# A two-layer graph network on one core: router logits in one product, one attention product moved behind the second aggregation, and a tail written tile by tile

## The reference

```python
# layer 0: gnn0 = diffusion over the edges, mix0 = linear attention, ffn0 = 16 experts, 2 per node
x = x + gnn0(ln(x)) + mix0(ln(x))
x = x + ffn0(ln(x))              # gates: softmax(ln(x) @ w_gating)
# layer 1
xn = ln(x)
h  = xn + elu(ln(gat_conv(xn, W1, 8 heads)))
g  = h  + elu(ln(gat_conv(h,  W2, 1 head)))      # gat_conv: segment softmax over the edges, then sum
q, k, v = split(xn @ W_qkv); q = softmax(q, features); k = softmax(k, nodes)
mix = (q @ (k.T @ v)) @ W_out + b_out            # per head; k.T @ v is the "context"
x = x + g + mix
x = x + ffn1(ln(x))              # 8 experts, 2 per node; gates: softmax(ln(x) @ Wr + br)
```

## Time and profile before

| | us |
|---|---|
| three runs | 227.12, 228.76, 228.8 |
| median | 228.76 |
| the profiled execution, whole | 225.84 |
| its span, first to last instruction | 224.1 |
| TensorE busy in it | 212.0 |

### The profile page before, as it was taken

How to read it: one execution, slowest core, us unless ns; L and a number is a source line. 1 busy time by engine, 2 the same in 40 slices (tenths; PEclk the granted TensorE clock), 3 DMA queues, 4 the chain that set the end, 5 groups by cost and what they waited for, 6 DMA issues and landing times.

```text
span 224.1 us, 2899 instructions
## 1 busy us (share of the span) xinstructions
PE 212.0 (95%) x1008; PEld 140.5 (63%) x1008; DVE 140.5 (63%) x416; ACT 63.9 (28%) x150; POOL 21.2 (9%) x36
## 2 busy tenths in 40 slices
PE   7999999998999999999999999999969999499994
PEld 5785546654579688744845686469754444359741
DVE  3799999968997151332519139696944749734302
ACT  2804594231311112100011139930563202104100
POOL 4850100000101000000140000000300002100000
PEclk9999999999999999999997999999999999999999
DMA  6999899924050500000079200000000000000002
GB/s 170 346 391 350 265 414 412 407 81 146 6 184 3 187 0 3 0 0 0 0 244 389 118 0 1 3 0 0 0 0 3 0 0 0 0 1 3 0 0 94
DMA packets 8957, 23.65 MB, mean 106 GB/s; under 512 B 2408, under 2 KB 2408, under 8 KB 8944
## 3 DMA queue, kind: packets, MB, share of 16 engines
q1 hardware_dynamic: 8656, 23.42, 28.9%
q10 hardware_dynamic: 288, 0.07, 0.1%
HBM read 22.95 MB, written 0.52 MB: 105 GB/s over the span
## 4 chain that ended last, share of the span: by engine, by line
PE 84%; DVE 11%; issue 2%; POOL 0%; ACT 0%; POOLq 0%; DVEq 0%
PE bank L1158 17%; PE bank L1132 13%; PE bank L1250 10%; PE bank L1262 9%; PE bank L1298 6%; PE bank L1207 3%; PE bank L1169 3%; PE bank L1213 3%; DVE ring L792 3%; PE bank L1312 2%; PE bank L1146 2%; PE bank L1214 2%; PE bank L1198 2%; DVE ring L795 2%; PE bank L1444 1%
## 5 line engine op out<-in xcount | busy, mean ns | idle before, releaser
L1158 PE MATMUL bank<-raw,xT 128*128 128x512 f32 x88 | 39.9, 602 | 0.0
L1158 PEld LDWEIGHTS bank<-raw,xT 128*128 128x128 f32 x88 | 16.7, 195 | 19.2 <-issue 19.0
L303 POOL TENSOR_TENSOR rstd<-veps,minus_half 128x1 f32<-128x1 f32 x14 | 8.4, 607 | 158.8 <-DVE veps L569 90.3
L1250 PE MATMUL bank<-xT,raw 128*128 128x256 f32 x96 | 22.7, 386 | 0.0
L1298 PE MATMUL bank<-iota_bf 128*128 128x256 bf16 x144 | 21.1, 300 | 1.6 <-DVE iota_bf L768 1.6
L1262 PE MATMUL bank<-raw,ring 128*128 128x512 f32 x48 | 21.0, 594 | 0.0
L792 DVE TENSOR_SCALAR ring<-iota_bf,edges,radix 128x128 bf16<-128x128 bf16 x64 | 20.0, 379 | 0.0
L1250 PEld LDWEIGHTS bank<-xT,raw 128*128 128x128 f32 x96 | 17.6, 190 | 3.1 <-issue 0.9
L1298 PEld LDWEIGHTS bank<-iota_bf 128*128 128x128 bf16 x144 | 15.5, 112 | 5.1 <-DVE iota_bf L768 1.6
L1262 PEld LDWEIGHTS bank<-raw,ring 128*128 128x128 f32 x48 | 9.0, 190 | 10.9 <-issue 10.5
L1207 PE MATMUL bank<-raw,yT 128*128 128x512 f32 x32 | 14.3, 595 | 0.7 <-issue 0.7
(11 more groups left out here) (255 smaller groups left out, 331.8 us busy)
## 6 DMA issues: line engine op xcount, KB each, us to landing
raw<-in_up SPq DMA_DIRECT2D x6, 512.0 KB, 10.3
raw<-in_down SPq DMA_DIRECT2D x6, 512.0 KB, 13.0
raw<-in_k SPq DMA_DIRECT2D x4, 512.0 KB, 6.0
raw<-in_q SPq DMA_DIRECT2D x4, 512.0 KB, 6.7
raw<-in_v SPq DMA_DIRECT2D x4, 512.0 KB, 7.9
raw<-in_out SPq DMA_DIRECT2D x4, 512.0 KB, 6.5
raw<-in_gat SPq DMA_DIRECT2D x4, 512.0 KB, 9.1
raw<-in_gnn SPq DMA_DIRECT2D x2, 512.0 KB, 11.4
```

The lines of the kernel that those rows point to most:

```text
L1158: ins = mm(bank[banks[t]][:, :], xT_at(c, t), w.at(c), start=c == 0, stop=c == C - 1)
L1250: ins = mm(half(m // 2, m % 2), w.at(c, m * P, (m + 1) * P), xT_at(c), start=c == 0, stop=c == C - 1)
```

## The change

1. **Gates of both layers.** `logit_rows`, the ScalarE copy and the transposes go. `logits` now makes the logits in their final form, one tile at a time: the transposed rows are the stationary operand, and the gate weights (16 or 8 columns) stream. For layer 0 tile 0 stands right behind `xT_made(1)`, then five idle turns, then tile 1; for layer 1 both stand behind the five idle turns that follow `xT_made(4)`.
2. **`attention_weights` of the second `gat_conv`.** Four products in all. Chunk 0 goes ahead of the first `attn_out` of layer 0, chunks 1 and 2 to the place where chunk 0 and nine idle turns stood, and chunk 3 stays behind the experts of layer 0, among idle turns of other counts.
3. **`context` and `yT_made` of layer 1** go from ahead of `xT_made(3)` to behind the second aggregation, with six idle turns behind each. On ScalarE the copies of `ctxbd` and `yT` go along, ahead of the exponentials of the second elu. `h2` now lives in `hx` and `mixed` of layer 1 in `q`, since `ek` and `v` are still needed.
4. **VectorE's tail of layer 1** is written tile by tile in another order, instead of both tiles in each step.

The diff, cut to its core:

```diff
-        h2 = ek
+        h2 = hx[:, :, :, :].rearrange("p t h n -> p t (h n)")[:, :, 0:D]
...
             elu(0, (0,))
-            act.wait_ge(ctx_full, 2)
-            for r in range(2):
-                p0, p1 = r * HD, (r + 1) * HD
-                copy(ctxbd[p0:p1, :, p0:p1], bank[3][p0:p1, :].rearrange("p (m n) -> p m n", m=C)[:, :, p0:p1])\
-                    .then_inc(ctx_ready, 1)
             elu(0, (1,))
-            yT_part(1, (5, 2))
             xT_part(3, 4)
...
                 copy(h2[:, t, :], bank[5 - t][:, :]).then_inc(hx_ready, 1)
+            act.wait_ge(ctx_full, 2)
+            for r in range(2):
+                p0, p1 = r * HD, (r + 1) * HD
+                copy(ctxbd[p0:p1, :, p0:p1], bank[4][p0:p1, :].rearrange("p (m n) -> p m n", m=C)[:, :, p0:p1])\
+                    .then_inc(ctx_ready, 1)
+            yT_part(1, (5, 4))
             elu(1)
             xT_part(4, 3)
-            lgT_part(1, 5)
...
-            go(V.scalar_tensor_tensor(mixed[:, :, :], x1g[:, :, :], -1.0, xa[:, :, :], ALU.add, ALU.add))
+            go(V.scalar_tensor_tensor(q[:, :, :], x1g[:, :, :], -1.0, xa[:, :, :], ALU.add, ALU.add))
...
+            def negative(t):
+                settle()
                 dve.wait_ge(elu_exp, T + t + 1)
+                go(V.scalar_tensor_tensor(q[:, t, :], g_b[:, t, :], 1.0, q[:, t, :], ALU.min, ALU.add))
...
+            def summed(t):
+                settle()
                 dve.wait_ge(o_full, 2 + t + 1)
+                go(V.tensor_tensor(xb[:, t, :], bank[t][:, :], q[:, t, :], ALU.add))
                 settle()
                 variance(6, t, xb[:, t, :])
...
+            scaled(0)
+            settle()
+            variance(5, 0, g_a[:, 0, :])
+            scaled(1)
+            centred(0)
+            normal(0)
+            variance(5, 1, g_a[:, 1, :])
+            centred(1)
+            positive(0)
+            normal(1)
+            negative(0)
+            summed(0)
+            positive(1)
+            negative(1)
+            norm_rows(6, xn[:, 0, :], xb[:, 0, :], 0)
+            summed(1)
+            norm_rows(6, xn[:, 1, :], xb[:, 1, :], 1)
...
-            def logit_rows(b, L, i):
...
+            def logits(b, L, i, tiles=range(T)):
                 E = EXPERTS[L]
+                for t in tiles:
+                    pe.wait_ge(xT_ready[t], i + 1)
+                    ins = product(bank[b][:, N + t * E:N + (t + 1) * E], lambda c: xT_at(c, t),
+                                  lambda c: (w_router if L else w_gate)[:, c, 0:E], C)
+                if t == T - 1:
+                    ins.then_inc(logits_full, 1)
...
             yT_made(0, (4, 5))
+            pe.wait_ge(small_in, SMALLS)
+            attention_weights(1, 6, 0)
...
             diffuse(1, (3, 4))
-            attention_weights(1, 6, 0)
-            idle_turns(5, 9)
+            attention_weights(1, 6, 1)
+            idle_turns(5, 1)
+            attention_weights(1, 6, 2)
+            idle_turns(5, 1)
...
-            idle_turns(2, 6)
             pe.wait_ge(wa_ready, 1)
-            logit_rows(6, 0, 1)
-            up("up0", 0, 1, (0, 1))
-            logits(6, 0)
+            logits(6, 0, 1, (0,))
+            idle_turns(2, 5)
+            logits(6, 0, 1, (1,))
+            up("up0", 0, 4)
...
-            attention_weights(1, 7, 1)
-            idle_turns(5, 5)
-            attention_weights(1, 7, 2)
-            idle_turns(5, 2)
+            idle_turns(5, 6)
+            attention_weights(1, 7, 3).then_inc(wa_full, 1)
+            idle_turns(5, 6)
             xT_made(2, xn, (4, 5), (0,))
-            attention_weights(1, 7, 3).then_inc(wa_full, 1)
+            idle_turns(5, 4)
             xT_made(2, xn, (4, 5), (1,))
...
             qT_made((4, 5))
+            pe.wait_ge(qT_ready, 2 + C)
+            xT_made(3, x1g, (4, 3), (0,))
             pe.wait_ge(ek_ready, 4)
-            context(3)
-            pe.wait_ge(ctx_ready, 4)
-            pe.wait_ge(qT_ready, 2 + C)
-            yT_made(1, (5, 2))
-            xT_made(3, x1g, (4, 3))
+            xT_made(3, x1g, (4, 3), (1,))
...
+            context(4)
+            idle_turns(0, 6)
+            pe.wait_ge(ctx_ready, 4)
+            yT_made(1, (5, 4))
+            idle_turns(0, 6)
             pe.wait_ge(yT_ready, 4)
             for t in range(T):
                 attn_out("out1", t).then_inc(o_full, 1)
-            idle_turns(4, 4)
+            idle_turns(4, 8)
             xT_made(4, xn, (3, 4), (0,))
```

More of the change, by code:

```diff
@@ L371, in yT_part @@
                         .then_inc(yT_ready, 1)
-            def lgT_part(L, b):
-                act.wait_ge(lgT_full, L + 1)
-                copy(lgT[0:EXPERTS[L], :], bank[b][0:EXPERTS[L], 0:N]).then_inc(lgT_ready, 1)
             def gate_exp(L):
@@ L436, in _ @@
             copy(wa[:, :, 0:2 * H], bank[6][:, 0:C * A2].rearrange("p (c n) -> p c n", c=C)[:, :, 0:2 * H])
-            copy(wa[:, 0, 2 * H:A2], bank[6][:, 2 * H:A2]).then_inc(wa_ready, 1)
-            lgT_part(0, 6)
+            copy(wa[:, 0:3, 2 * H:A2], bank[6][:, 0:C * A2].rearrange("p (c n) -> p c n", c=C)[:, 0:3, 2 * H:A2])\
+                .then_inc(wa_ready, 1)
             gate_exp(0)
@@ L473, in _ @@
             act.wait_ge(wa_full, 2)
-            copy(wa[:, 1:C, 2 * H:A2], bank[7][:, 0:C * A2].rearrange("p (c n) -> p c n", c=C)[:, 1:C, 2 * H:A2])\
-                .then_inc(wa_ready, 1)
+            copy(wa[:, 3, 2 * H:A2], bank[7][:, 3 * A2 + 2 * H:4 * A2]).then_inc(wa_ready, 1)
             xT_part(2, 4)
@@ L1088, in _ @@
                     .then_inc(weight_ready, 1)
-            go(V.scalar_tensor_tensor(mixed[:, :, :], x1g[:, :, :], -1.0, xa[:, :, :], ALU.add, ALU.add))
+            go(V.scalar_tensor_tensor(q[:, :, :], x1g[:, :, :], -1.0, xa[:, :, :], ALU.add, ALU.add))
             settle()
-            go(V.tensor_tensor(mixed[:, :, :], mixed[:, :, :], row["b_out1"].unsqueeze(1).broadcast_to([P, T, D]),
+            go(V.tensor_tensor(q[:, :, :], q[:, :, :], row["b_out1"].unsqueeze(1).broadcast_to([P, T, D]),
                                ALU.add))
@@ L1097, in _, with scaled @@
             settle()
-            for t in range(T):
+            def scaled(t):
                 dve.wait_ge(agg_full, 4 + t + 1)
@@ L1101, in _, with centred, normal, positive @@
                                           ALU.mult, ALU.add))
-            gat_norm(1, 5)
-            for t in range(T):
+            def centred(t):
+                go(V.scalar_tensor_tensor(g_a[:, t, :], g_a[:, t, :], mv[:, t, 0:1], row["g2"],
+                                          ALU.subtract, ALU.mult))
+                settle()
+            def normal(t):
+                dve.wait_ge(rstd_ready, T * 5 + t + 1)
+                V.scalar_tensor_tensor(g_a[:, t, :], g_a[:, t, :], rstd[:, t:t + 1], row["beta2"],
+                                       ALU.mult, ALU.add).then_inc(y_ready, 1)
+            def positive(t):
                 dve.wait_ge(y_ready, T + t + 1)
-                go(V.scalar_tensor_tensor(mixed[:, t, :], g_a[:, t, :], 0.0, mixed[:, t, :], ALU.max, ALU.add))
-            for t in range(T):
-                settle(T - 1)
+                go(V.scalar_tensor_tensor(q[:, t, :], g_a[:, t, :], 0.0, q[:, t, :], ALU.max, ALU.add))
+            def negative(t):
+                settle()
                 dve.wait_ge(elu_exp, T + t + 1)
-                go(V.scalar_tensor_tensor(mixed[:, t, :], g_b[:, t, :], 1.0, mixed[:, t, :], ALU.min, ALU.add))
-            for t in range(T):
-                settle(T - 1 if t == 0 else 0)
+                go(V.scalar_tensor_tensor(q[:, t, :], g_b[:, t, :], 1.0, q[:, t, :], ALU.min, ALU.add))
+            def summed(t):
+                settle()
                 dve.wait_ge(o_full, 2 + t + 1)
-                go(V.tensor_tensor(xb[:, t, :], bank[t][:, :], mixed[:, t, :], ALU.add))
+                go(V.tensor_tensor(xb[:, t, :], bank[t][:, :], q[:, t, :], ALU.add))
                 settle()
                 variance(6, t, xb[:, t, :])
-                norm_rows(6, xn[:, t, :], xb[:, t, :], t)
+            scaled(0)
+            settle()
+            variance(5, 0, g_a[:, 0, :])
[13 more added lines that the diff above has]
+            norm_rows(6, xn[:, 1, :], xb[:, 1, :], 1)
             xT_part(4, 4)
@@ L1544, in _ @@
             idle_turns(6, 5)
[L1545 to L1549, removed]
+            logits(5, 1, 4)
+            up("up1", 0, 2)
             up("up1", 2, 3, (0, 1))
```

5 lines of the change are left out of this document (removed).

## The result

| | before | changed |
|---|---|---|
| median, us | 227.94 (20 runs) | 228.56 (20 runs) |
| lowest and highest | 223.90, 230.50 | 226.53, 242.11 |
| changed / before | | 1.0084, 95% interval 1.0043 to 1.0125 |

The forecast was 227.5 us, faster by 0.6%; by the ratio the kernel is slower, and only the range held the time.

A forecast was written before the change was run, and what follows sets the result against it. TensorE, busy for 212.0 of 224.1 us, was taken as the bound. The terms -0.93 - 0.92 - 0.33 - 1.83 + 2.70 = -1.31 us, put on the median of 228.76, gave 227.5 us; range 225.0 to 230.4.

The forecast's parts named there:

- gates of layer 0: From xT_made(1) to positions, 16 streamed columns per tile and fewer up instructions after them save 0.93 us.
- gates of layer 1: After xT_made(4), both tiles behind the five idle turns, the wait for xT disappearing under tile 0: 0.92 us saved.
- `attention_weights`: Ahead of xT_made(2), products and fewer idle turns let the normed tile 1 decide: 0.33 us saved.
- context out of the middle, clock up: Ahead of xT_made(3), 4.74 us leave TensorE's list, node rows come 1.83 us earlier, and a 2.6 us wait remains.
- context into the tail: Between second aggregation and xT_made(4), product, copies and turns of 5.6 us replace a 3.15 us wait: 2.70 us lost.
- the clock at the new wait: Ahead of xT_made(3), the 2.6 us wait costs nothing, since full clock followed the 3.15 us wait in the tail.
- Chunk 0 at nothing: Its 0.81 us product stands in TensorE's wait for layer 0's yT copies; loss between 0 and 0.81, taken as 0.
- chunks 1 and 2: With two idle turns they cost 1.84 us, as much as chunk 0 and nine idle turns: no loss.
- attention decided: In the tail of layer 1, attention and no longer VectorE's norm sets the time, so VectorE's new order buys nothing.
- rival 3: VectorE decides in the tail, so the product there is free: at best -4.0 us, 224.8 us; chance 0.05.
- rival 1: Clock falls at the new wait ahead of xT_made(3) and stays down: one fall 229.2 us, two 230.9; chance 0.2.
- Rival 2: In the median runs a fall behind the tail's long wait goes with that wait: 225.8 us, 1.3% faster; chance 0.2.

The follow-up runs named there:

- the repeat: The changed kernel with nothing altered, run and profiled again beside the kernel before: 226.95 us median, ratio 1.0053.
- the products back: The changed kernel with the four attention_weights of the second gat_conv where they were before: 227.03 us, ratio 1.0028.
- experiment 1: Changed kernel run again: 226.95 us, ratio 1.0053; with 22 idle turns in the wait ahead of xT_made(3) and six behind: 226.48 us, 0.9835.
- the gates-only kernel: The changed kernel with context and attention_weights back in their old places, leaving the new gates and VectorE's new tail: 224.65 us, ratio 0.9877.
- experiment 3: Kernel before with the context move only: 229.2 us, ratio 1.0131; with the moved attention_weights only: 228.51 us, ratio 1.0132.
- experiment 5: Idle turns in TensorE's own waits, added to new gates and VectorE tail only: 224.02 us, ratio 0.9898; to the kernel before: 225.93 us, 1.0004.
- experiment 4: Changed kernel with attention_weights back: 227.03 us, ratio 1.0028; also with idle turns: 224.51, 0.9882; with context and attention_weights both back: 224.65, 0.9877.

## Why the prediction was wrong

| term | forecast, us | measured, us | from |
|---|---|---|---|
| gates of layer 0 | -0.93 | -1.13 | 10.72 to 9.59 |
| gates of layer 1 | -0.92 | -1.04 | 8.13 to 7.09 |
| `attention_weights` | -0.33 | -0.34 | 3.63 to 3.29 |
| context out of the middle, clock up | -1.83 | -1.74 | 7.55 to 5.81 |
| context into the tail | +2.70 | +2.71 | 10.63 to 13.34 |
| sum | -1.31 | -1.54 | |
| the clock at the new wait | 0 | +2.9 | 12.58 against 9.68 |
| in all | -1.31 | +1.36 | |

Every move was sized within 0.2 us. Chunk 0 at nothing held too: from `yT_made` to the first `attn_out` of layer 0 TensorE's timeline has 2.63 us in the kernel before (48.74 to 51.37) and 2.63 in the repeat (48.57 to 51.20). So did chunks 1 and 2: the stretch from the diffusion step ahead of them to the folded products took 4.28 us in both (61.99 to 66.27, and 61.83 to 66.11). In the tail attention decided, as worked out, and rival 3 fell: VectorE's norm ends no wait there.

**The step that failed** is the sentence "By that row the new wait of 2.6 us costs nothing; it goes into the sum with that", and with it the chance of 0.2 for rival 1. Its mechanism is what happened; its price of 1.7 for one fall and 3.4 for two in a row encloses the 2.9, while the shorter fall in the trace with the products back cost 1.34. With 2.9 the sum is +1.36 us, 0.6% of the kernel's time, inside the measured 0.4 to 1.25%. That agreement is no proof of the size, since the executions of both kernels also differ by falls at other places (experiment 1). The row taken for evidence was a wait of 3.15 us followed by the upper level, and two waits in these runs still agree with it: 2.45 us in the tail of the gates-only kernel has 1.00 behind it, and so has the wait of 3.16 us in the trace of the moved products alone (experiment 3). But directly ahead of those stand 7 us of `attn_out` and idle turns, and directly ahead of the new one 2.0 us of transposes; whether that makes the difference was not tried. What was shown is that the length of a wait was the wrong thing to carry over from one place to another.

The page that was set aside, the Trainium skill, "TensorE: Matmul & The Clock Gate", section "Why this matters for your kernels", asks for no idle gap over a certain length between bursts of matmuls, and has TensorE back at half clock behind such a gap. The middle went the way that the prediction drew from it, with a loss of 2.9 instead of 1.7 us and a sum of +1.36 instead of +0.4. But the traces do not bear out a rule by length: behind the wait of 2.69 us the clock fell, and behind the longer one of 3.15 us it stood at 1.00.

**Rival 2**, that filling the tail gives back a fall, may hold for a part of the executions: turns in the waits of before took its longer ones away (experiment 5), and which of its three waits did that is open. It gave the changed kernel no time below the sum of the terms: at its best, with the middle filled, it ran in 222.29 us and before in 223.76 in the same set, 1.5 us apart. The forecast also stood on a median of three runs, 0.8 above that of twenty, which no term of it could answer for.

**Is the context move worth it with turns?** By its terms no: -1.74 + 2.71 at a full clock, and it costs VectorE's 0.72 in the tail. In the measured times the versions with and without it can't be told apart (experiment 4). Gates and tail alone, 0.9877, or the whole with turns and the products back, 0.9882, beat both kernels, on six executions each.

## What to carry to other kernels

Before work is moved out of a place where it fills a wait, price the wait that it leaves at the lower clock: up to half of the stretch that runs until the clock rises again, here 1.3 to 2.9 us. Put idle turns into that wait in the same step: here they gave back 2.9 us in the wait behind which the clock fell, and in the waits of the kernel before, where the trace shows no fall, they cost nothing (ratio 1.0004) and made its longer executions rarer. A row that shows a wait without a fall is evidence for that place, with what stands ahead of it, and for no other.

## What was not expected of the hardware

- A wait of 2.69 us brought the granted clock to 0.50 in each of the four traces that have it open with no turns (3.3 to 6.8 us low) and in the one with turns behind (3.15 us); waits of 3.15 and 2.45 us in the tail did not.
- In layer 0 the clock fell behind products of two columns and stayed at 0.50 through 22 us without idle time (66 to 88 us, products of 16 columns, idle turns and the first expert products). With eight more idle turns ahead of it, at 0.30 us, none of twelve executions was long.
- The gates of layer 0 gained little by the exchange of the operands itself. Stationary transposed rows with 16 gate columns streamed took 0.81 us for one tile (73.39 to 74.20), so 1.62 for both; 16 stationary columns with 256 streamed, which is both tiles, took 1.82 to the next start (74.58 to 76.40). That is 0.20 of the 1.13 us. The rest is the wait and an idle turn less, no transposes, and one group of `up` in place of two.
